# Attention 0 of a two-layer cross-attention block: VectorE spreads the turned maxima, the last unit sums more on TensorE, and waits for tables move to their use

## The reference

```python
x = x + _L0_xattn_ref(_layernorm(x), ctx_2048, ...)            # 16 heads of 32, int8 fake-quantised projections
x = x + _L0_ffn_ref(_layernorm(x), W1, W2)                     # 512 -> 2048 -> 512, gelu of a rounded code
x = x + _L1_xattn_ref(_layernorm(x), ctx_2048, mask_BxS2_ik0, ...)  # scores clipped to +-50, masked
x = x + _L1_ffn_ref(_layernorm(x), W_up, W_down, W_gate, W_expert)
# attention of layer 0
attn = jax.nn.softmax(jnp.einsum('bnhd,bmhd->bhnm', q, k) * scale, axis=-1)
o = jnp.einsum('bhnm,bmhd->bnhd', attn, v).reshape(B, N, C)
out = _qdq(o) @ _qdq(wp).T + bp
# attention of layer 1
scores = jnp.clip(scores, -50.0, 50.0)
scores = jnp.where(attend, scores, -10000.0)
scores = jnp.clip(scores, -50.0, 50.0)
```

## Time and profile before

| | |
|---|---|
| median of 3 runs | 2897.01 us (2891.08 to 2897.37) |
| the profiled execution's own time | 2894.31 us |
| its span, first to last instruction | 2892.5 us |
| TensorE (PE) busy | 2617.3 us (90%) |
| VectorE (DVE) busy | 1774.1 us (61%) |
| ScalarE (ACT) busy | 1276.1 us (44%) |
| GpSimd (POOL) busy | 1254.0 us (43%) |
| mean granted TensorE clock | 0.955 of full speed |

### The profile page before, as it was taken

How to read it: one execution, slowest core, us unless ns; L and a number is a source line. 1 busy time by engine, 2 the same in 40 slices (tenths; PEclk the granted TensorE clock), 3 DMA queues, 4 the chain that set the end, 5 groups by cost and what they waited for, 6 DMA issues and landing times. The chain is left out here.

```text
span 2892.5 us, 35367 instructions
## 1 busy us (share of the span) xinstructions
PE 2617.3 (90%) x13977; PEld 1682.9 (58%) x13992; DVE 1774.1 (61%) x2500; ACT 1276.1 (44%) x1904; POOL 1254.0 (43%) x319
## 2 busy tenths in 40 slices
PE   8999999969999999999956999998899999992898
PEld 7888888854444444444414777786334333332776
DVE  4554545427565665656505566554899999994664
ACT  3222312103666566666641222222688878782211
POOL 1000000024998898989870000000677777773010
PEclk9999999987999999999987999999999999996999
DMA  8666656454533425244016333335877777713110
GB/s 292 214 233 230 247 219 234 180 163 93 107 74 79 102 61 117 64 87 94 16 37 247 102 102 124 112 105 153 188 154 155 154 154 153 153 36 117 54 48 29
DMA packets 205973, 382.17 MB, mean 132 GB/s; under 512 B 16072, under 2 KB 91880, under 8 KB 205808
## 3 DMA queue, kind: packets, MB, share of 16 engines
q1 hardware_dynamic: 205808, 379.92, 47.3%
HBM read 247.92 MB, written 131.94 MB: 131 GB/s over the span
## 5 line engine op out<-in xcount | busy, mean ns | idle before, releaser
L994 DVE TENSOR_REDUCE win_max<-psum 128x1 f32<-128x802 f32 x512 | 484.6, 987 | 300.7 <-PE psum L849 299.8
L1056 POOL TENSOR_TENSOR pooled<-pooled,probs 128x2048 f32<-128x2048 f32 x144 | 658.0, 4570 | 21.3 <-ACT probs L957 0.5
L957 ACT ACTIVATE probs<-psum 128x512 f32<-128x512 f32 (+1 forms) x832 | 459.3, 598 | 300.6 <-PE psum L881 297.2
L1721 DVE TENSOR_SCALAR probs<-psum,bound 128x1024 f32<-128x1024 f32 (+1 forms) x416 | 508.0, 1277 | 43.9 <-PE psum L1618 43.9
L1676 ACT ACTIVATE probs<-probs 128x1024 f32<-128x1024 f32 (+1 forms) x416 | 440.8, 1060 | 114.4 <-DVE probs L1721 77.9
L1756 POOL TENSOR_TENSOR pooled<-pooled,probs 128x2048 f32<-128x2048 f32 x80 | 368.4, 4605 | 79.6 <-ACT probs L1676 79.6
L881 PE MATMUL psum<-q_st,k_st 128*128 128x512 f32 (+1 forms) x832 | 341.3, 442 | 55.0 <-ACT probs L957 32.5
L849 PE MATMUL psum<-k_st,q_st 96*128 96x402 f32 x1024 | 301.0, 379 | 33.1 <-DMA q_st<-q_lo 23.9
L881 PEld LDWEIGHTS psum<-q_st,k_st 128*128 128x128 f32 (+1 forms) x832 | 151.0, 186 | 279.7 <-ACT probs L957 187.0
L189 POOL TENSOR_TENSOR r_q<-ve_q,minus_half 128x4 f32<-128x4 f32 x8 | 8.1, 1011 | 660.7 <-DVE ve_q L165 660.7
L1618 PE MATMUL psum<-q_st,k_st 128*128 128x512 f32 (+1 forms) x832 | 250.2, 422 | 11.6 <-DVE ones L1729 11.0
(11 more groups left out here) (253 smaller groups left out, 4102.4 us busy)
## 6 DMA issues: line engine op xcount, KB each, us to landing
k_st<-k_hi SPq DMA_DIRECT2D x64, 801.0 KB, 14.8
k_st<-k_lo SPq DMA_DIRECT2D x48, 801.0 KB, 11.2
k_hi<-kt_hi SPq DMA_DIRECT2D x32, 801.0 KB, 3.6
k_lo<-kt_lo SPq DMA_DIRECT2D x32, 801.0 KB, 5.7
v_rows<-v_out SPq DMA_DIRECT2D x96, 256.0 KB
v_st<-v_rows SPq DMA_DIRECT2D x24, 768.0 KB
q_st<-q_hi SPq DMA_DIRECT2D x64, 256.0 KB, 11.2
w<-w_hi_d SPq DMA_DIRECT2D x64, 256.0 KB, 2.6
```

The source lines that it names most:

```text
L957: A.activation(probs[i % NPROBS][0:rows, j, :], bank(score_banks.where["score", u, t, j])[0:rows, :], ACT.Exp, scale=1.0 / ROOT).then_inc( ...
L994: V.tensor_reduce(win_max[:, r, j, c:c + 1], window(windows.where["max", u, i])[:, :, 0:MV], AX.XY, ALU.max).then_inc(max_done, 1)
L1056: G.tensor_tensor(pooled[u % 2][:], before[:], probs[tile(u, POOLED[k]) % NPROBS][:], ALU.add).then_inc(pool_added, 1)
L1721: V.tensor_scalar(probs[i % NPROBS][0:rows, half * W:half * W + W, :], window(("score", u, t, half))[0:rows], bound[0:rows, u // NG, t:t + 1],
```

## The change

- In attention 0 the copies of the turned maxima go from ScalarE (`turn`) to VectorE (`spread`), in the same step.
- The number of pooled tiles becomes `pooled_tiles(u)`: 11 as before, and 7 in the last unit. There GpSimd makes 6 additions instead of 10, TensorE sums tiles 7 to 10 as well, and the third score bank is used in steps 4 to 8 instead of 4 to 12.
- In the feed-forward stage the wait for `tables` moves from the start of TensorE's and VectorE's programs to the first product of the projection and to the first instruction that reads them.
- The mask is loaded in the feed-forward stage, as a part of `q_tables` (now four transfers), and VectorE computes `bound` there, behind its wait for them.
- In attention 1 the load of the mask and the two instructions go, and TensorE waits for `ones` at its first sum instead of ahead of its first score.

```diff
@@ attention_0 @@
-            POOLED = list(range(11))
-            FIRST_SUM, LAST_SUM, THREE = 11, 1, range(4, TT)
+            LAST_SUM = 1
...
+                def three_banks(u, t):
+                    return 4 <= t < pooled_tiles(u) + LAG
...
+                def pooled_tiles(u):
+
+                    return 11 if u < UNITS - 1 else 7
+
                 def adds(u):
-                    return u * (len(POOLED) - 1)
+                    return sum(pooled_tiles(v) - 1 for v in range(u))
...
-                        slot, free = score_banks.take(("score", u, t, j), among=(0, 1, 7) if t in THREE else (0, 1))
+                        slot, free = score_banks.take(("score", u, t, j), among=(0, 1, 7) if three_banks(u, t) else (0, 1))
...
-                        if t in POOLED:
+                        if t < pooled_tiles(u):
                             m.then_inc(tile_read, 1)
                             return
...
-                        if t == FIRST_SUM:
+                        if t == pooled_tiles(u):
...
-                    def turn(u):
-                        A.wait_ge(turned_ps, u + 1)
-                        for j in range(0, HPG, 2):
-                            A.activation(q_st[u % NSLOT][96:128, j:j + 2, :],
-                                         window(windows.where["turn", u])[96:128, 0:1, :].to_broadcast([DH, 2, S]),
-                                         ACT.Copy).then_inc(turned, 1)
-
-                    turn(0)
...
-                        if now and now[1] == TURN_AT and now[0] + 1 < UNITS:
-                            turn(now[0] + 1)
...
+                    def spread(u):
+                        V.wait_ge(turned_ps, u + 1)
+                        for j in range(0, HPG, 2):
+                            V.tensor_copy(q_st[u % NSLOT][96:128, j:j + 2, :],
+                                          window(windows.where["turn", u])[96:128, 0:1, :].to_broadcast([DH, 2, S])
+                                          ).then_inc(turned, 1)
...
                     turn(0)
+                    spread(0)
...
                         if now and now[1] == TURN_AT - 1 and now[0] + 1 < UNITS:
                             turn(now[0] + 1)
+                        if now and now[1] == TURN_AT and now[0] + 1 < UNITS:
+                            spread(now[0] + 1)
...
-                        for k in range(1, len(POOLED)):
-                            G.wait_ge(exp_done, score(u, POOLED[k], HPG))
+                        for k in range(1, pooled_tiles(u)):
+                            G.wait_ge(exp_done, score(u, k, HPG))
...
@@ ffn_0_and_q_projection_1: TensorE @@
                             if r == 0:
+                                M.wait_ge(tables, 16 * 3)
                                 M.wait_ge(q_turned, (b + 1) * KT)
...
-                    M.wait_ge(tables, 16 * 3)
                     for _ in projected(0):
...
@@ ScalarE @@
-                    A.wait_ge(q_tables, 16 * 3)
+                    A.wait_ge(q_tables, 16 * 4)
...
@@ VectorE @@
                             V.wait_ge(y_ps, i + 1)
+                            if i == 0:
+                                V.wait_ge(tables, 16 * 3)
...
-                    V.wait_ge(tables, 16 * 3)
                     for _ in projected(0):
                         pass
                     operand(0)
-                    V.wait_ge(q_tables, 16 * 3)
+                    V.wait_ge(q_tables, 16 * 4)
+                    s = own.after(V.tensor_scalar(bound[:], mask_i[:], 0.5, 100.0 * ROOT, ALU.is_gt, ALU.mult))
+                    V.wait_ge(own.sem, s)
+                    V.tensor_scalar(bound[:], bound[:], 50.0 * ROOT, None, ALU.subtract)
...
@@ SyncE @@
                     load(bq[:], a["bq1"], q_tables)
+                    load(mask_i[:], a["mask_t"], q_tables)
                     for h, src in enumerate((wq_hi_d, wq_lo_d)):
...
@@ attention_1 @@
                             if t == FIRST_SUM and u:
                                 M.wait_ge(den_copied, u)
+                            elif t == FIRST_SUM:
+                                M.wait_ge(set_up, 1)
...
-                    M.wait_ge(set_up, 1)
...
-                    V.wait_ge(mask_landed, 16)
-                    s = own.after(V.tensor_scalar(bound[:], mask_i[:], 0.5, 100.0 * ROOT, ALU.is_gt, ALU.mult))
-                    V.wait_ge(own.sem, s)
-                    V.tensor_scalar(bound[:], bound[:], 50.0 * ROOT, None, ALU.subtract)
                     V.memset(ones[:], 1.0).then_inc(set_up, 1)
...
-                    load(mask_i[:], a["mask_t"], mask_landed)
                     load_v(1)
```

More of the change, by code:

```diff
@@ L824, in windows_at @@
                     return range(min(t * WINDOWS, HPG * RT * 2), min((t + 1) * WINDOWS, HPG * RT * 2))
+                def pooled_tiles(u):
+                    return 11 if u < UNITS - 1 else 7
                 def adds(u):
-                    return u * (len(POOLED) - 1)
+                    return sum(pooled_tiles(v) - 1 for v in range(u))
                 def pool_reads(u, t):
-                    return adds(u) + max(POOLED.index(t), 1)
+                    return adds(u) + max(t, 1)
                 def steps():
@@ L905, in values @@
                             m = M.matmul(den[j * DH:(j + 1) * DH, :], ones[0:rows, :], pr[0:rows, j, :],
-                                         start=(t == FIRST_SUM), stop=False)
+                                         start=(t == pooled_tiles(u)), stop=False)
                         m.then_inc(tile_read, 1)
@@ L952, in exps @@
                             pu, pt = divmod(i - NPROBS, TT)
-                            if pt in POOLED:
+                            if pt < pooled_tiles(pu):
                                 A.wait_ge(pool_added, pool_reads(pu, pt))
@@ L1051, in pool_program @@
                                     G.wait_ge(summed, u - 1)
-                                before = probs[tile(u, POOLED[0]) % NPROBS]
+                                before = probs[tile(u, 0) % NPROBS]
                             else:
@@ L1055, in pool_program @@
                                 before = pooled[u % 2]
-                            G.tensor_tensor(pooled[u % 2][:], before[:], probs[tile(u, POOLED[k]) % NPROBS][:],
+                            G.tensor_tensor(pooled[u % 2][:], before[:], probs[tile(u, k) % NPROBS][:],
                                             ALU.add).then_inc(pool_added, 1)
@@ L1101, in attention_0, with ffn_0_and_q_projection_1 @@
                 close()
-        def ffn_0_and_q_projection_1(early_k, x_hi, x_lo, v_view):
+        def ffn_0_and_q_projection_1(early_k, x_hi, x_lo, v_view, mask_i, bound):
             with ExitStack() as scope:
@@ L1209, in queries @@
                                 M.wait_ge(xq_lo_done, (b + 1) * KT)
-                                M.wait_ge(q_tables, 16 * 3)
+                                M.wait_ge(q_tables, 16 * 4)
                             terms = []
@@ L1523, in advance, with attention_1 @@
                 next(side, None)
-        def attention_1(early_k, early_q, early_v):
+        def attention_1(early_k, early_q, early_v, bound):
             n, NQ = 1, 4
@@ L1542, in attention_1 @@
                 acc, den = bank(6), bank(7)
-                mask_i, bound = sbuf("mask_i", [P, B, TT], I32), sbuf("bound", [P, B, TT])
                 own = Chain(sem("dve_own"))
-                set_up, mask_landed = sem("set_up"), sem("mask_landed")
+                set_up = sem("set_up")
                 kq_landed = [sem(f"kq_landed{s}") for s in range(NG)]
@@ L2145, in build @@
             v_view = f32(early_v[:]).rearrange("p k s -> p (k s)")[:, 0:TT * P].rearrange("p (t c) -> p t c", c=P)
-            ffn_0_and_q_projection_1(early_k, early_q, early_v, v_view)
-            attention_1(early_k, early_q, v_view)
+            mask_i, bound = sbuf("mask_i", [P, B, TT], I32), sbuf("bound", [P, B, TT])
+            ffn_0_and_q_projection_1(early_k, early_q, early_v, v_view, mask_i, bound)
+            attention_1(early_k, early_q, v_view, bound)
         out_projection_and_ffn_1()
```

## The result

The changed kernel takes **2848.88 us** (median, 2847.8 to 2851.05) against 2895.24 us of the kernel before, run beside it (2891.08 to 2897.37). The ratio is 0.9843, with a 95% interval from 0.9825 to 0.9860: 46.4 us less. The forecast was 2852, with a range of 2843 to 2865. The profiled execution took 2848.65 us, 45.7 less than the profiled one of before; its span is 2846.9 us and its mean granted clock 0.961.

What follows compares the result with a forecast made beforehand. TensorE, busy 90% of the span, was taken as the bound; 21.9 - 0.3 + 9.0 + 8.9 + 1.7 + 2.1 = 43.3 us off the profiled 2894.31 gave 2851.0, plus 1: 2852 us, range 2843 to 2865.

Steps and rivals of the forecast that it cites:

- The turn: Turn inside attention 0: without ScalarE's copies TensorE's next unit starts 1.46 us earlier, 21.9 us for 15 turns.
- The clock: Attention 0: six long units lose their drops to 1.2 GHz behind the turn's idle time, 9.0 us, bounds 0 and 9.
- The 0.3 us lost ahead of the first addition: Turn of unit 0: nothing covers VectorE's copy, 1.28 us against ScalarE's 0.97, so 0.3 us are lost.
- GpSimd as the bound: Rival, attention 0: copies hold GpSimd back 2.6 us a pair, units 49.6 us, 7 us lost, 2858; chance 0.06.
- The last unit: Attention 0's last unit: last sum 7.1 us earlier without the wait for GpSimd, it and transposes at full clock; 8.9 us.
- The start of the feed-forward stage: VectorE's first reduction 3.5 us earlier, partly taken over by the q_tables wait: 1.7 us gained, bounds 0.5 and 3.5.
- The start of attention 1: TensorE's first score no longer waits behind the mask and `ones` after the barrier: 2.1 us.

## Why the prediction was right, and where it was off

- **The turn**, 21.9 us. The usual distance fell from 50.59 to 49.08, 1.51 a turn against 1.46. Right, with the copy at 1.22 us against 1.28 taken.
- **The clock**, 9.0 us. Six long units of 1.5 us went. The units' step in the table is 31.8 us; without the 8.9 of the six drops, 22.9 are left for the 15 turns (21.9 forecast). Right, at the upper bound of its 0 to 9; that idle time is the cause was argued then and is shown now. The 0.3 us lost ahead of the first addition can't be told from the scatter there. The Trainium skill ("TensorE: Matmul & The Clock Gate", section "Why this matters for your kernels") names only long unbroken gaps between bursts of matmuls as what to avoid. This trace does not agree: in the run with doubled copies waits of 0.49 and 1.12 us have low clock behind them at seven of 15 turns.
- **GpSimd as the bound**: 42.33 against 42.27 us, so no copy held it back, and it idles 2 us a unit. The Trainium skill ("SBUF — State Buffer", section "SBUF: two separate sides") gives the lock that VectorE and GpSimd share to VectorE instructions in a two-port mode or with two SBUF inputs. The prediction took it that a copy out of PSUM is neither, and the trace agrees.
- **The last unit**, 8.9 us: 8.6 in the table, and 8.6 in the run of this part alone. Behind the unit's first addition the last sum starts 6.9 us earlier (7.1 forecast), and runs 0.9 us shorter.
- **The start of the feed-forward stage**, 1.7 us. This is the term with the wrong working. VectorE went on 2.7 us earlier against the end of attention 0, not 1.7: I had set the end of the `q_tables` wait 0.9 us too late. But 1.6 us of that are lost again by attention 1's barrier, where I had the cost of the wait end with VectorE's start. In its place the profiles show TensorE's gap grown from 2.46 to 4.56 us and the low clock under its work behind it from 3.4 to 5.9 us; at half clock that is 1.2 of the 1.6 us. It is worth 5.8 us to be rid of the wait. The stage's gain over before, 1.1 us in this pair of profiles, is no firm number. From the reciprocal to attention 1's barrier the four profiles without the moved waits take 525.6 to 527.6 us, and the seven with them as in the changed kernel 524.5 to 526.8. That the forecast's 1.7 us are near 1.1 says nothing for its working.
- **The start of attention 1**, 2.1 us: 2.15.
- The sum was 43.3 us up to attention 1's first score, where the profiles show 43.0. The last 2.6 us of the profiled difference come behind it, and are luck: from that score to the end the 13 profiles take 853.8 to 858.0 us, and the pair compared here has 857.2 before and 854.6 after. They are also why the profiled execution, at 2848.65 us, came out below the 2851.0 of the sum.

## What to carry to other kernels

Price idle time of TensorE at its length and what the clock takes behind it: here a turn with 1.98 us of waits instead of 0.45 cost 3.1 us a unit, and over two fifths of that was clock. Look for it as units of two lengths and read the granted clock in windows of 1 us right behind the wait. And when a wait moves to where a table is used, move it to the instruction that reads the table, not to the head of the stretch that holds it: the engine's other work queues behind the wait, and so does TensorE.

## What the runs showed of the hardware

- The granted clock fell to the 1.2 GHz level behind waits of 1.23 and 0.52 us (6 of 15 turns in the kernel before; 6, 6 and 7 in the three other kernels with its turn), 1.45 and 0.53 (9), 0.49 and 1.12 (7), 2.53 and 0.28 (15), and not behind 0.45, nor behind 0.36 and 0.52 (0 of 15 each). Within one execution some of these like turns had the low clock behind them and others not. What decides between them stays open.
- A drop came in two sizes, 1.5 and 3.1 us of lost time; with 2.53 and 0.28 us of waits all 15 turns had the larger, and with 1.45 and 0.53 us four of nine. With the waits of before it came once, in the run of the moved waits alone (a distance of 53.7 us).
- VectorE's copy of 1,024 elements on 32 partitions from PSUM took 1.22 us, with the clip of 128 partitions at 1.28; ScalarE's took 0.97.
